# A scan, top-2 routing, an expert layer and its combination: three program blocks or one

## The chip, the cores and the metric

The kernel runs on one core of a Trainium2 chip. The metric is device time in microseconds (us) of one launch. The kernel before took 756.34 us, the median of three runs (754.75 to 756.58).

## The reference

The computation has five parts. The first two thirds of the time (a gated scan over 128 steps, relative-position attention with 16 heads, its output projection) are the same in both kernels. The changed part is the rest:

```python
# x: (32, 128, 128) after attention and residual; T = 128 steps, N = 32*128 = 4096 tokens, D = 128
xp = einsum('ntd,dh->nth', x, Wx) + b
h_t = tanh(xp_t + h_{t-1} @ Wh)                  # second scan, 128 steps, 32 sequences
p = softmax(h @ router_w.T)                      # 8 experts
w, idx = top_k(p, 2);  w = w / (w.sum() + 1e-9)
y_e = gelu(h @ W1_e.T + b1_e) @ W2_e.T + b2_e    # 128 -> 512 -> 128, exact gelu, expert e
out = x + sum over the two chosen e of w_e * y_e
```

Everything is float32.

## The kernel before, in words

A kernel is written as blocks. In a block each engine has its own instruction stream, and streams meet through semaphores. At the end of a block every engine executes a drain (listed on the line of the block, as L824) and then waits at a barrier for all others. The changed part is three blocks.

**Block 1 (L824 to L1047): second scan and routing.** The 128 steps are cut into 8 chunks of 16 steps, which are 512 tokens each. TensorE and ScalarE alternate on the scan: four matmul pairs by `wh2`, then a tanh (L918). While chunk m is scanned, chunk m-1 is routed: TensorE makes its logits and its transposed rows (L861), VectorE picks the two experts of each token, weighs them (L995 to L1002), counts positions per expert (L1008) and writes 8 columns of slot numbers, `slotu` (L1016). GpSimd then issues 8 scatters (L940), each of 128 rows of 129 floats (a token's state and the number of its output row) to its slot in the DRAM array `expert_inputs`. Each expert has its own region there. Per chunk:

```python
for k in range(2 * JT):
    pool.indirect_dma_start(xg_dram, ..., rows[o][:, k, :], None).then_inc(s_sc, 16)
pool.wait_ge(s_sc, (c + 1) * (16 * 2 * JT))
pool.sem_inc(s_scd, 1)
```

The wait (L942) and the increment (L943) let VectorE overwrite the row buffer. There are two buffers, `rows0` and `rows1`. After the eighth chunk VectorE makes the table of tiles `tab` (L1029 to L1047), and SP (the queue of the sync engine) writes 8 pieces of padding behind the experts' last rows (L847 to L852), one by one with a register load for each.

**Block 2 (L1082 to L1210): experts.** 72 tiles of 128 rows. A register load from `tab` gives the first row of a tile and its expert. SP loads the tile's rows into one of 8 buffers `xr` (L1090). TensorE transposes them (L1106), multiplies by the first weights (L1113) and by the second (L1130). ScalarE copies the expert's first weights (L1153) and does the gelu (L1144). VectorE copies the second weights (L1194) and adds the bias into `yr` (L1210). GpSimd scatters the 128 result rows to `expert_outputs` (L1173), at the row numbers that came with the tokens. The program has 8 tiles written out, a loop of 7 passes over 8 tiles, and 8 tiles written out again. The block ends when GpSimd has seen all scatters land (L1178 and L1179).

**Block 3 (L1221 to L1262): combination.** For each of 8 chunks SP loads both choices' results (two loads of 256 KB, L1231), VectorE adds them with their weights to the residual (8 operations, L1244), and ScalarE's queue writes 256 KB of output (L1260). A partition p holds the tokens j*128 + p of a chunk, so every row of these transfers is one token of 512 bytes.

The parts that the change touches, and what calls them:

Of the kernel before, what the change touches and what calls it, by code (L numbers as in the profile page):

```python
# [6 lines left out]
U32 = mybir.dt.uint32  # L7
I32 = mybir.dt.int32
ALU = mybir.AluOpType
# [3 lines left out]
P = 128  # L13
# [19 lines left out]
NS = 72  # L33
# [7 lines left out]
def build(nc, a):  # L41


    with ExitStack() as ctx:
# [760 lines left out]
        s_sc = sem("rows_scattered")  # L805
        s_scd = sem("chunk_scattered")
# [6 lines left out]
        VLINKS = 18  # L813

# [4 lines left out]
        def chunks(step):  # L819

            for m in range(NCH + 1):
                step(m, m < NCH, m >= 1)

        with nc.Block() as block:  # L824
            @block.sync
            def _(sp):
# [25 lines left out]
                sp.wait_ge(s_fill, 16 * E)  # L852

            @block.tensor
            def _(pe):
# [14 lines left out]
                def step(m, scan_on, route_on):  # L870
# [6 lines left out]
                    for j in range(TC):  # L877
# [9 lines left out]
                        if 2 <= j < 2 + JT:  # L887
                            k = j - 2
                            if k == 0:
                                pe.wait_ge(s_slot, c + 1)  # L890
                            tile = h2[o][:].rearrange("p t b -> p (t b)")[:, k * P:(k + 1) * P]
                            mm = column_products(2, k * E, (k + 1) * E, tile, rwT[:])
                            if k == JT - 1:
                                mm.then_inc(s_lg, 1)
                            mm = column_products(3, k * P, (k + 1) * P, tile, ident[:])
                            if k == JT - 1:
                                mm.then_inc(s_rt, 1)
                        if j == 12:
# [7 lines left out]
            @block.scalar  # L906
            def _(act):
                act.sem_inc(s_h2, 1)
                act.preload_act_table_set("exp_and_others")
                act.wait_ge(s_c2, 16)  # L910

                def step(m, scan_on, route_on):
                    r = m % 2
                    for j in range(TC):
                        if scan_on:
                            t = m * TC + j
                            act.wait_ge(s_r, t + 1)
                            act.activation(h2[r][:, j, :], ps[r][:, j * B:(j + 1) * B], ACT.Tanh,  # L918
                                           bias=cols[:, 5:6]).then_inc(s_h2, 1)
                        if route_on and j == 9:  # L920
                            act.wait_ge(s_ea, m)
                            act.activation(ex[:], lg[:], ACT.Exp).then_inc(s_eb, 1)

                chunks(step)

            @block.gpsimd
            def _(pool):
                pool.sem_inc(s_scd, 2)
                pool.wait_ge(s_rin, 144)
                pool.memset(ones[:], 1.0)  # L930
                pool.memset(pad[:, :, 0:D], 0.0)
                pool.tensor_copy(pad[:, :, D].bitcast(U32), padid[:]).then_inc(s_pad, 1)

                def step(m, scan_on, route_on):
                    if not route_on:
                        return
                    c, o = m - 1, 1 - m % 2
                    pool.wait_ge(s_slot, c + 2)
                    for k in range(2 * JT):
                        pool.indirect_dma_start(xg_dram, bass.IndirectOffsetOnAxis(slotu[o][:, k:k + 1], 0),  # L940
                                                rows[o][:, k, :], None).then_inc(s_sc, 16)
# [3 lines left out]
                chunks(step)  # L945

            @block.vector
            def _(dve):
                dve.sem_inc(s_slot, 1)
                dve.wait_ge(s_rin, 144)  # L950
                dve.wait_ge(s_pad, 1)
                dve.tensor_copy(offs[:, 0, :], ebase[:]).then_inc(s_init, 1)
                dve.wait_ge(s_init, 1)

                def step(m, scan_on, route_on):
                    if not route_on:
                        return
                    c, o = m - 1, 1 - m % 2
                    k = [0]

                    def link(op):
                        k[0] += 1
                        op.then_inc(s_v, 1)
                        dve.wait_ge(s_v, c * VLINKS + k[0])

                    def over_e(v):
                        return v.unsqueeze(len(v.shape)).broadcast_to([*v.shape, E])

                    dve.wait_ge(s_lg, c + 1)
                    link(dve.tensor_copy(lgc[:], ps[2][:, 0:JT * E].rearrange("p (j e) -> p j e", e=E)))  # L970
                    dve.tensor_reduce(small[:, 0, :], lgc[:], AX.X, ALU.max)
                    for j in range(JT):
                        op = dve.max(top[:, j, :], lgc[:, j, :])
                    link(op)

                    dve.tensor_tensor(lg[:], lgc[:], over_e(small[:, 0, :]), ALU.subtract).then_inc(s_ea, 1)
                    for j in range(JT):
                        op = dve.max_index(topi[:, j, :], top[:, j, :], lgc[:, j, :])
                    link(op)
                    link(dve.tensor_copy(topf[:], topi[:]))  # L980
                    for x in range(2):
                        op = dve.tensor_tensor(sel[:, x], iota[:].unsqueeze(1).broadcast_to([P, JT, E]),
                                               topf[:, :, x:x + 1].broadcast_to([P, JT, E]), ALU.is_equal)
                    link(op)
                    dve.tensor_tensor(both[:], sel[:, 0], sel[:, 1], ALU.add).then_inc(s_sel, 1)

                    dve.wait_ge(s_rt, c + 1)
                    dve.wait_ge(s_scd, c + 1)
                    for x in range(2):
                        dve.tensor_copy(rows[o][:, x * JT:(x + 1) * JT, 0:D], ps[3][:].rearrange("p (j d) -> p j d", d=D))  # L990
                    link(dve.tensor_copy(rows[o][:, :, D].bitcast(U32), destf[:]))
                    link(dve.tensor_scalar(destf[:], destf[:], float(BANK), None, ALU.add))

# [322 lines left out]
```

## Time and profile before

| | us |
|---|---|
| median of three runs | 756.34 |
| the profiled execution, its own time | 756.94 |
| its span, first to last instruction | 755.1 |
| TensorE busy in the span | 577.0 |
| VectorE, ScalarE, GpSimd busy | 428.5, 402.4, 394.1 |
| block 1: span from | 443.1 |
| block 2: span from | 574.6 |
| block 3: span from | 727.5 |

Times in the trace are microseconds from the start of the span. Busy times are sums over instructions and do not say what waits for what. An instruction with a letter q behind its engine (POOLq, SPq) is a sequencer's: a drain, a semaphore or the issue of a transfer. The end of a scatter on GpSimd (POOL) is the end of its issue; its landing comes later and is listed apart. A row of a source line gives the instruction, how often it ran, its shortest, median and longest duration in ns, and the start of the first and the last.

### The profile page before, as it was taken

The numbers are of one execution on the slowest core, as the hardware profiler recorded it, in microseconds if no ns is written. First come the engines' busy times: TensorE is split into PE (matmuls) and PEld (weight loads), VectorE is DVE, ScalarE is ACT, GpSimd is POOL, SyncE is SP. The second block draws the span as 40 slices with busy tenths as digits, with TensorE's granted clock in tenths as the row PEclk, the third lists the DMA queues.
The fourth block names the chain that finished last, engine by engine and source line by source line (L and its number), as shares of the span: only waits on it lengthen the run. The fifth ranks groups of instructions, "written<-read, shape, count | busy, mean of one in ns | idle before, by whom it ended". The sixth has DMA issues, their size and how long they took to land. (4 is left out here: it accounts for less than half of the span.)

```text
span 755.1 us, 26992 instructions
## 1 busy us (share of the span) xinstructions
PE 577.0 (76%) x10048; PEld 442.5 (59%) x10048; DVE 428.5 (57%) x1998; ACT 402.4 (53%) x1129; POOL 394.1 (52%) x436
## 2 busy tenths in 40 slices
PE   3888888888679989999999666776403999999900
PEld 1655565565556666667767433333203999999900
DVE  1666666666357678777785423645631555555517
ACT  4666666666205555555556243444203999999800
POOL 3454454455148688888886101656660555555510
PEclk9999999999979999999999785756555999999955
DMA  6365565565756666676653027111121222222238
GB/s 238 131 232 200 205 230 191 189 231 189 251 145 193 183 186 195 178 195 193 197 170 115 1 69 229 48 42 45 44 74 36 68 70 68 70 70 70 57 106 235
DMA packets 124140, 106.41 MB, mean 141 GB/s; under 512 B 9216, under 2 KB 100864, under 8 KB 123776
## 3 DMA queue, kind: packets, MB, share of 16 engines
q1 hardware_dynamic: 115456, 93.88, 40.0%
q0 software_dynamic: 4352, 8.95, 3.6%
q10 hardware_dynamic: 4224, 2.10, 0.9%
q8 instruction: 73, 1.20, 0.7%
q14 instruction: 35, 0.29, 0.2%
HBM read 57.15 MB, written 45.65 MB: 136 GB/s over the span
## 5 line engine op out<-in xcount | busy, mean ns | idle before, releaser
L473 POOL TENSOR_TENSOR sc<-sc,mx 128x1024 f32<-128x1024 f32 x64 | 121.3, 1897 | 55.6 <-DVE mx L613 55.6
L383 POOL TENSOR_SCALAR QD<-q_all,mask 128x128 f32<-128x128 f32 x128 | 89.5, 712 | 98.3 <-DVE pre L348 95.0
L613 DVE CUSTOM_DVE_ANT_0 sc<-banks,s2t 128x128 f32<-128x128 f32 x512 | 113.0, 286 | 47.1 <-PE banks L523 46.8
L1173 POOL DMA_INDIRECT expert_outputs<-yr,xr x72 | 72.1, 1001 | 80.0 <-DVE yr L1210 75.2
L662 ACT ACTIVATE PT<-banks 128x512 f32<-128x512 f32 x128 | 69.7, 595 | 76.6 <-PE banks L538 76.3
L940 POOL DMA_INDIRECT expert_inputs<-rows,slotu x64 | 61.9, 967 | 52.5 <-DMA expert_inputs<-rows,slotu 19.6
L339 DVE COPY s2stage<-banks 128x512 f32<-128x512 f32 (+1 forms) x90 | 76.6, 852 | 16.5 <-PE banks L248 16.5
L1144 ACT ACTIVATE hid<-banks,w1b 128x128 f32<-128x128 f32 x288 | 82.3, 369 | 4.2 <-PE banks L1113 4.2
L248 PE MATMUL banks<-RK,QD 32*128 32x128 f32 x1024 | 78.5, 454 | 4.0 <-DVE s2stage L339 0.9
L1113 PE MATMUL banks<-xt,w1b 128*128 128x128 f32 x576 | 77.8, 279 | 0.0
L1130 PE MATMUL banks<-w2b,hid 128*128 128x128 f32 x576 | 76.4, 276 | 0.3 <-ACT hid L1144 0.3
L538 PEld LDWEIGHTS banks<-ident,sc 128*128 128x128 f32 x512 | 55.5, 142 | 29.5 <-issue 19.7
L1113 PEld LDWEIGHTS banks<-xt,w1b 128*128 128x128 f32 x576 | 71.7, 196 | 0.0
L538 PE MATMUL banks<-ident,sc 128*128 128x128 f32 x512 | 70.7, 281 | 0.5 <-issue 0.5
L1130 PEld LDWEIGHTS banks<-w2b,hid 128*128 128x128 f32 x576 | 70.4, 193 | 0.5 <-ACT hid L1144 0.5
L348 DVE TENSOR_TENSOR_SCAN pre<-xz,gl 128x64 f32<-128x64 f32 x128 | 37.5, 293 | 53.8 <-ACT gl L300 50.6
L215 PEld LDWEIGHTS banks<-hs,wh 128*32 128x32 f32 x1016 | 25.6, 140 | 71.0 <-ACT hs L303 71.0
L248 PEld LDWEIGHTS banks<-RK,QD 32*128 32x128 f32 x1024 | 61.1, 318 | 9.8 <-issue 6.6
L918 ACT ACTIVATE h<-banks,cols 128x32 f32<-128x32 f32 x128 | 36.8, 288 | 56.1 <-PE banks L861 56.1
L215 PE MATMUL banks<-hs,wh 128*32 128x32 f32 x1016 | 42.6, 251 | 28.7 <-ACT hs L303 25.4
L861 PE MATMUL banks<-h,wh 128*32 128x32 f32 x1024 | 40.0, 236 | 30.5 <-ACT h L918 30.4
L1194 DVE TENSOR_SCALAR w2b<-w2all 128x640 f32 x72 | 38.6, 536 | 42.7 <-issue 42.1
(121 smaller groups left out, 1001.5 us busy)
## 6 DMA issues: line engine op xcount, KB each, us to landing
s_scratch<-s2stage SPq DMA_DIRECT2D x32, 1024.0 KB, 4.9
s2t<-s_scratch SPq DMA_DIRECT2D x64, 512.0 KB, 4.6
xr<-expert_inputs SPq DMA_DIRECT2D x72, 64.5 KB, 1.8
xz<-in_xz SPq DMA_DIRECT2D x8, 512.0 KB, 5.9
yb<-expert_outputs SPq DMA_DIRECT2D x16, 256.0 KB, 4.8
KB<-k_all SPq DMA_DIRECT2D x32, 64.0 KB, 3.4
q_all<-in_xT SPq DMA_DIRECT2D x1, 2048.0 KB, 9.0
w1a<-in_w1T SPq DMA_DIRECT2D x1, 2048.0 KB, 8.8
```

What stands on the lines that cost most here:

```text
L215: mm = pe.matmul(ps[bank][at, lo:hi], w[:, at], moving, start=first, stop=last, tile_position=(0, 32 * c), skip_group_check=True)
L248: mm = pe.matmul(ps[4 + j][:, tl * T:(tl + 1) * T], QD[G % 3][32 * j:32 * j + 32, tl].rearrange("p h b -> p (h b)"), relk_window(j, t), st ...
L339: dve.tensor_copy(stage[G % SETS][:, lo:hi].rearrange("p g q k -> p (g q k)"), banks[:, (4 + lo) * BANK:(4 + hi) * BANK]).then_inc(s_s2c, 1)
L383: op = pool.tensor_scalar(QD[G % 3][:, :, h, :], q_all[:, :, quad(G)].rearrange("p b t -> p t b"), mask[:, h:h + 1], None, ALU.mult)
L473: pool.tensor_tensor(sc[U % RING][:], sc[U % RING][:], mx[U % RING][:].unsqueeze(2).broadcast_to([P, HH, T]), ALU.subtract)\
L538: mm = pe.transpose(blocked[:, j // 2, j % 2], sc[U % RING][:, 4 * x + j, :], ident[:])
L613: op = dve.tensor_tensor_reduce(out=sc[r][:, h, :], in0=ps[2 * (U % 2) + h // 4][:, h % 4 * T:(h % 4 + 1) * T], in1=s2t[r][:, h, :], scale ...
L662: act.activation(pairs[:, 2 * (2 * u + x):2 * (2 * u + x) + 2], ps[4 + x][:].rearrange("p (a r) -> p a r", a=2), ACT.Exp, scale=DH ** -0.5 ...
L1113: mm = pe.matmul(ps[2 + k % 2][:, f * P:(f + 1) * P], w1b[k % 2][:, f * P:(f + 1) * P], xt[k % 2][:], start=True, stop=True)
L1130: mm = pe.matmul(ps[4 + k % 2][:, 0:D], hid[k % 2][:, f, :], w2b[k % 2][:, f * D:(f + 1) * D], start=(f == 0), stop=(f == FC - 1))
L1144: op = act.activation(hid[k % 2][:, f, :], ps[2 + k % 2][:, f * P:(f + 1) * P], ACT.Gelu, bias=w1b[k % 2][:, FF + f:FF + f + 1])
L1173: pool.indirect_dma_start(yg_dram, bass.IndirectOffsetOnAxis(xr[k][:, D:].bitcast(U32), 0), yr[k][:], None).then_inc(s_ys[k], 16)
```

## The change

- The three blocks become one. Where a block ended, engines now wait for semaphores: SP waits for all padding, all scatters and the table before it loads the first tile, and for all result scatters before it loads the first results.
- GpSimd no longer waits for a chunk's scatters. `rows_scattered` becomes two semaphores, one for each row buffer, and VectorE waits for the scatters of the chunk before the last one when it reuses the buffer.
- For the last chunk the order changes: TensorE makes the four logits ahead of the four transposed rows; ScalarE copies the rows; VectorE computes the slots, then the table, and only then the weights of the two choices.
- ScalarE's queue issues four of the eight paddings. Its gelu table is loaded behind the scan.
- 71 tiles in place of 72. The last seven are written out behind the loop.
- A partition now holds tokens 4p to 4p+3 of a chunk at the end: `destf` numbers the output rows so, each partition's row of a combination transfer is 2 KB in one piece, and the host puts the token order right by a transpose.

```diff
-NS = 72
+NS = 71
-        s_sc = sem("rows_scattered")
-        s_scd = sem("chunk_scattered")
+        s_sc = [sem(f"rows_scattered{i}") for i in range(2)]
...
             @block.sync
             def _(sp):
...
                 sp.wait_ge(s_end, 1)
                 sp.sem_inc(s_spass2, 1)
-                for e in range(E):
-                    end = sp.value_load(ends[0:1, e:e + 1], min_val=0, max_val=E * CAP - P)
-                    sp.dma_start(xg_dram[bass.ds(end, P), :], pad[:, e, :]).then_inc(s_fill, 16)
+                for e in range(0, E, 2):
+                    fill(sp, e)
                 sp.wait_ge(s_fill, 16 * E)
+                for o in range(2):
+                    sp.wait_ge(s_sc[o], NCH // 2 * 16 * 2 * JT)
+                sp.wait_ge(s_tab, TLINKS)
...
+                for k in range(RX - 1):
+                    load(NS // RX, k, True)
+
+                for k in range(RX):
+                    sp.wait_ge(s_ys[k], 16 * (NS // RX + (k < NS % RX)))
+                yin = yg_dram[0:2 * N, :].rearrange("(x c p j) d -> c x p j d", x=2, j=JT, p=P)
...
             @block.tensor
...
+                            if scan_on:
+                                logits(j - 2)
+                                rows_of(j - 2)
+                            elif j == 2:
+                                for k in range(JT):
+                                    logits(k)
+                                for k in range(JT):
+                                    rows_of(k)
...
             @block.scalar
...
+                        if route_on and not scan_on and j == 8:
+                            act.wait_ge(s_last, 1)
+                            act.wait_ge(s_rt, m)
+                            for x in range(2):
+                                op = act.activation(rows[1 - r][:, x * JT:(x + 1) * JT, 0:D],
+                                                    ps[3][:].rearrange("p (j d) -> p j d", d=D), ACT.Copy)
+                            op.then_inc(s_rows, 1)
...
+                act.preload_act_table_set("gelu_and_others")
+                act.wait_ge(s_end, 1)
+                act.sem_inc(s_apass2, 1)
+                for e in range(1, E, 2):
+                    fill(act, e)
+                act.wait_ge(s_tab, TLINKS)
+                act.wait_ge(s_win, 16 * (3 + E))
...
             @block.gpsimd
...
                     pool.wait_ge(s_slot, c + 2)
+                    if not scan_on:
+                        pool.wait_ge(s_rows, 1)
                     for k in range(2 * JT):
                         pool.indirect_dma_start(xg_dram, bass.IndirectOffsetOnAxis(slotu[o][:, k:k + 1], 0),
-                                                rows[o][:, k, :], None).then_inc(s_sc, 16)
-                    pool.wait_ge(s_sc, (c + 1) * (16 * 2 * JT))
-                    pool.sem_inc(s_scd, 1)
+                                                rows[o][:, k, :], None).then_inc(s_sc[o], 16)
...
-                for k in range(RX):
-                    pool.wait_ge(s_ys[k], 16 * (NS // RX))
...
             @block.vector
...
+                    def last_rows():
+                        dve.wait_ge(s_sc[o], c // 2 * 16 * 2 * JT)
+                        dve.tensor_copy(rows[o][:, :, D].bitcast(U32), destf[:]).then_inc(s_last, 1)
...
+                    if scan_on:
+                        state_rows()
+                        weights()
+                        slots()
+                    else:
+                        slots()
+                        dve.wait_ge(s_slot, c + 2)
+                        table()
+                        weights()
+                        return
...
-        "dest": (np.arange(2)[None, :, None] * N + np.arange(JT)[None, None, :] * P
-                 + np.arange(P)[:, None, None]).reshape(P, 2 * JT).astype(np.float32),
+        "dest": (np.arange(2)[None, :, None] * N + np.arange(JT)[None, None, :]
+                 + np.arange(P)[:, None, None] * JT).reshape(P, 2 * JT).astype(np.float32),
```

How the instructions stand, at three places. First GpSimd from the sixth chunk's scatters to the first result scatter, before (a line is a source line, the operation, what it writes and reads, and the semaphores that it waits for):

```order
L940 DMA expert_inputs<-rows1,slotu1 34816x129 [waits rows_scattered,rows_and_slots_ready]
L940 DMA expert_inputs<-rows1,slotu1 34816x129 x7
L940 DMA expert_inputs<-rows0,slotu0 34816x129 [waits rows_scattered,rows_and_slots_ready]
L940 DMA expert_inputs<-rows0,slotu0 34816x129 x7
L940 DMA expert_inputs<-rows1,slotu1 34816x129 [waits rows_scattered,rows_and_slots_ready]
L940 DMA expert_inputs<-rows1,slotu1 34816x129 x7
L824 UNCONDITIONAL_BRANCH [waits rows_scattered]
L1168 UNCONDITIONAL_BRANCH [waits barrier_Pool_Activation_PE_DVE_SP_gather]
L1173 DMA expert_outputs<-yr0,xr0 10240x128 [waits tile_outputs_ready]
```

and in the changed kernel:

```order
L1121 DMA expert_inputs<-rows1,slotu1 34688x129 [waits rows_and_slots_ready]
L1121 DMA expert_inputs<-rows1,slotu1 34688x129 x7
L1121 DMA expert_inputs<-rows0,slotu0 34688x129 [waits rows_and_slots_ready]
L1121 DMA expert_inputs<-rows0,slotu0 34688x129 x7
L1121 DMA expert_inputs<-rows1,slotu1 34688x129 [waits last_state_rows_copied,rows_and_slots_ready]
L1121 DMA expert_inputs<-rows1,slotu1 34688x129 x7
L1129 DMA expert_outputs<-yr0,xr0 10112x128 [waits tile_outputs_ready]
```

The wait for `rows_scattered` at each chunk and the branch with the barrier are gone; the last chunk waits for ScalarE's copy of the rows.

Second, SP from the last tile load to the first load of results, before:

```order
L1090 DMA xr7<-expert_inputs 128x129
L1094 REGISTER_ALU
L1094 COMPARE_AND_BRANCH
L1082 UNCONDITIONAL_BRANCH
L1222 UNCONDITIONAL_BRANCH [waits barrier_Pool_Activation_PE_DVE_SP_release]
L1225 UNCONDITIONAL_BRANCH
L1225 ISA
L1231 ISA [waits second_choice_added]
L1231 DMA yb0<-expert_outputs 128x4x128
```

and in the changed kernel:

```order
L906 DMA xr6<-expert_inputs 128x129
L919 UNCONDITIONAL_BRANCH [waits tile_outputs_scattered4,tile_outputs_scattered5,tile_outputs_scattered3,tile_outputs_scattered6,tile_outputs_scattered2,tile_outputs_scattered7,tile_outputs_scattered1,tile_outputs_scattered0]
L919 ISA
L925 ISA [waits second_choice_added]
L925 DMA yb0<-expert_outputs 128x512
```

The barrier's release is replaced by waits for the scatters themselves, and a load's rows are 512 floats in one piece.

Third, VectorE behind the last chunk's choices, before:

```order
L985 TENSOR_TENSOR both<-sel 128x32 [waits routing_chain]
L990 COPY rows1<-banks 128x4x128 [waits chunk_scattered,state_rows_ready]
L990 COPY rows1<-banks 128x4x128
L991 CAST rows1<-destf 128x8
L992 TENSOR_SCALAR destf<-destf 128x8 [waits routing_chain]
L995 TENSOR_REDUCE small<-ex 128x4 [waits router_exp_ready,routing_chain]
L996 TENSOR_TENSOR exs<-sel,ex 128x64
L997 TENSOR_REDUCE er<-exs 128x8 [waits routing_chain]
L998 TENSOR_TENSOR small<-er 128x4 [waits routing_chain]
```

and in the changed kernel:

```order
L1242 TENSOR_TENSOR both<-sel 128x32 [waits routing_chain]
L1215 TENSOR_TENSOR offs<-offs,banks 128x8 [waits positions_ready]
L1215 TENSOR_TENSOR offs<-offs,banks 128x8 [waits routing_chain] x3
L1216 TENSOR_TENSOR pos<-banks,offs 128x32 [waits routing_chain]
L1218 COPY offs<-offs 128x8 [waits routing_chain]
L1219 TENSOR_TENSOR exs<-sel,pos 128x64
L1220 TENSOR_REDUCE slotf<-exs 128x8 [waits routing_chain]
L1222 CAST slotu1<-slotf 128x8 [waits slot_numbers_ready]
L1152 CAST ends<-offs 128x8 [waits rows_and_slots_ready]
```

The copies of the rows have left VectorE, and the weights (L995 to L1002 before) stand behind the table.

## Rows read from the trace of the kernel before

**Rows 1.** Windows: stretch; busy PE, PEld, DVE, ACT, POOL; clock; DMA share, GB/s

```profile
569.00:575.00 6.00, 0.00 (x0) 0.00 (x0) 0.00 (x0) 0.23 (x1) 0.00 (x0) 0.50 0.00 0
583.00:718.00 135.00, 134.42 (x1203) 134.03 (x1202) 72.31 (x211) 124.27 (x353) 70.76 (x71) 1.00 0.25 67
718.00:728.00 10.00, 0.00 (x0) 0.00 (x0) 0.09 (x1) 0.00 (x0) 1.31 (x2) 0.57 0.05 14
```

**Rows 2.** Lines L943, L824; timeline (start, length, instruction): the first block's end

```profile
L943 POOLq EVENT_SEMAPHORE  x8: 17/17/17, 481.1 to 569.1; - x8
...
L824 POOLq DRAIN  x1: 5280/5280/5280, 569.2 to 569.2; - x1
L824 SPq EVENT_SEMAPHORE  x1: 17/17/17, 574.6 to 574.6; - x1
...
575.41 8.09 SPq L1090 DMA_DIRECT2D xr<-expert_inputs  x8
```

**Rows 3.** Line L1082: the second block's end

```profile
L1082 POOLq DRAIN  x1: 5943/5943/5943, 721.4 to 721.4; - x1
L1082 SPq EVENT_SEMAPHORE  x1: 17/17/17, 727.5 to 727.5; - x1
```

**Rows 4.** Timeline, GpSimd's scatters; in brackets the idle time ahead

```profile
469.21 1.18 POOL L940 DMA_INDIRECT expert_inputs<-rows,slotu  x1 [15.85 <-DVE slotu L1016]
...
541.67 0.96 POOL L940 DMA_INDIRECT expert_inputs<-rows,slotu  x1 [0.30 <-issue]
544.76 0.95 POOL L940 DMA_INDIRECT expert_inputs<-rows,slotu  x1 [2.13 <-DMA expert_inputs<-rows,slotu]
...
551.07 1.36 POOL L940 DMA_INDIRECT expert_inputs<-rows,slotu  x1 [0.31 <-issue]
...
566.78 0.96 POOL L940 DMA_INDIRECT expert_inputs<-rows,slotu  x1 [0.30 <-issue]
```

**Rows 5.** Timeline around the last two chunks: VectorE and SP

```profile
537.94 0.17 DVE L1016 CAST slotu<-slotf 128x8 uint32<-128x8 f32 x1
...
540.95 0.19 DVE L970 COPY lgc<-banks 128x32 f32<-128x32 f32 x1 [2.84 <-PE banks L861]
...
548.84 0.17 DVE L1016 CAST slotu<-slotf 128x8 uint32<-128x8 f32 x1
...
550.39 8.41 SPq L851 DMA_DIRECT2D expert_inputs<-pad  x8
...
554.30 0.23 DVE L1047 CAST tab<-tabf 128x144 int32<-128x144 f32 x1
```

**Rows 6.** Line L940 of the source, all 64 scatters: idle time, times

```profile
  DMA expert_inputs<-rows,slotu: 19.6, 7
...
DMA to landing us min/median/max: 2.3/2.3/3.7
```

**Rows 7.** Windows of 1 us behind the first tile (clock: third number from the end)

```profile
581.00:582.00 1.00, 1.00 (x7) 1.00 (x7) 0.46 (x2) 0.88 (x5) 0.00 (x0) 0.50 0.23 54
...
583.00:584.00 1.00, 1.00 (x11) 1.00 (x11) 0.30 (x2) 0.88 (x5) 0.00 (x0) 1.00 0.29 66
```

**Rows 8.** Timeline, the results of two tiles, one after the other

```profile
636.78 0.29 DVE L1210 TENSOR_TENSOR yr<-banks,w2b 128x128 f32<-128x128 f32 x1 [0.27 <-PE banks L1130]
...
638.68 0.29 DVE L1210 TENSOR_TENSOR yr<-banks,w2b 128x128 f32<-128x128 f32 x1 [0.27 <-PE banks L1130]
```

**Rows 9.** Timeline of the combination

```profile
727.95 15.74 SPq L1231 DMA_DIRECT2D yb<-expert_outputs  x16
732.03 1.14 DVE L1244 SCALAR_TENSOR_TENSOR x1r<-yb,wts,x1r 128x128 f32 x4 [13.94 <-DMA yb<-expert_outputs]
...
735.42 1.14 DVE L1244 SCALAR_TENSOR_TENSOR x1r<-yb,wts,x1r 128x128 f32 x4 [0.96 <-DMA yb<-expert_outputs]
```

**Rows 10.** Windows: the combination's loads, and the weights' loads in block 1

```profile
727.90:744.00 16.10, 0.00 (x0) 0.00 (x0) 10.21 (x37) 0.00 (x0) 0.00 (x0) 0.50 0.93 262
...
450.00:460.00 10.00, 6.37 (x152) 3.26 (x152) 0.17 (x1) 3.96 (x14) 2.11 (x3) 0.50 1.04 357
```

More of the change, by code:

```diff
@@ L813, in build @@
         VLINKS = 18
+        TLINKS = 10
         def before(r, j):
@@ L904, in _ @@
                 chunks(step)
[L906 to L940, printed above, removed]
-                                                rows[o][:, k, :], None).then_inc(s_sc, 16)
-                    pool.wait_ge(s_sc, (c + 1) * (16 * 2 * JT))
-                    pool.sem_inc(s_scd, 1)
-                chunks(step)
@@ L1082, in build @@
-        with nc.Block() as block:
-            @block.sync
-            def _(sp):
-                def load(i, k, reused):
-                    first = sp.value_load(tab[0:1, 1, bass.ds(i * RX + k, 1)], min_val=0, max_val=E * CAP + (NULL - 1) * P)
-                    if reused:
-                        sp.wait_ge(s_ys[k], i * 16)
-                        sp.sem_inc(s_lpass, 1)
-                    sp.dma_start(xr[k][:], xg_dram[bass.ds(first, P), :]).then_inc(s_xr[k], 16)
-                for k in range(RX):
-                    load(0, k, False)
-                with sp.Fori(1, NS // RX) as i:
-                    for k in range(RX):
-                        load(i, k, True)
-            @block.tensor
-            def _(pe):
@@ L1166, in _, with step @@
                 over_tiles(act, step)
+                with act.Fori(0, NCH // 2) as i:
+                    for r in range(2):
+                        c = i * 2 + r
+                        act.wait_ge(s_o1, c + 1 + RY)
+                        act.sem_inc(s_apass, 1)
+                        act.dma_start(a["out"].rearrange("(c p j) d -> c p j d", j=JT, p=P)[bass.ds(c, 1)]
+                                      .rearrange("c p j d -> (c p) j d"), x1r[:, bass.ds(c * JT, JT), :])\
+                           .then_inc(s_out[r], 16)
+                for r in range(2):
+                    act.wait_ge(s_out[r], 16 * (NCH // 2))
             @block.gpsimd
             def _(pool):
+                pool.wait_ge(s_rin, 144)
+                pool.memset(ones[:], 1.0)
+                pool.memset(pad[:, :, 0:D], 0.0)
+                pool.tensor_copy(pad[:, :, D].bitcast(U32), padid[:]).then_inc(s_pad, 1)
+                def step(m, scan_on, route_on):
+                    if not route_on:
+                        return
+                    c, o = m - 1, 1 - m % 2
+                    pool.wait_ge(s_slot, c + 2)
+                    if not scan_on:
+                        pool.wait_ge(s_rows, 1)
+                    for k in range(2 * JT):
+                        pool.indirect_dma_start(xg_dram, bass.IndirectOffsetOnAxis(slotu[o][:, k:k + 1], 0),
+                                                rows[o][:, k, :], None).then_inc(s_sc[o], 16)
+                chunks(step)
                 def step(i, k, s, has_next, has_second):
@@ L1182, in _ @@
+                chunks(step)
+                dve.wait_ge(s_win, 16 * (3 + E))
                 dve.sem_inc(s_xt, 2)
```

333 lines of the change are left out of this document (177 added, 156 removed).

## The prediction

> **What bounds the kernel now.** I read the windows first. Between 583 and 718 TensorE is busy 134.42 of 135 us at the full granted clock of 1.00: the expert tiles are bound by TensorE, and only fewer tiles or a start at another time can move that stretch. Ahead of it and behind it lie stretches in which nothing is busy: 569 to 575, and 718 to 728 but for 1.3 us of GpSimd [rows 1]. They are the place to look. Then I asked the timeline and the source lines what stands in them. At 569.1 the last of eight semaphore increments behind the scatters passes (L943): all rows have landed. GpSimd's sequencer then shows a drain that lasts 5.28 us, SP passes the barrier at 574.6, and the first tile load is issued at 575.41 [rows 2]. The second hole has the same form: a drain on GpSimd from 721.4 for 5.94 us, release at 727.5 [rows 3].
>
> What is ahead of 569.1 is GpSimd's stream of scatters, at 469.21 to 566.78 [rows 4]. It is the last thing that block 1 finishes: VectorE's table is ready at 554.53 and SP's paddings are issued by 558.8 [rows 5]. In this stream one scatter starts 1.26 us after the other (544.76 to 551.07 is five of them), and seven times GpSimd waits 2.1 us or more for a landing, 19.6 us in all [rows 4, 6]. So the critical path of this third of the program is: scan, slots, scatters, landing, drain, tiles on TensorE, last scatter's landing, drain, combination.
>
> **The change part by part.**
>
> *No wait per chunk.* The 19.6 us don't all come back, since the slots of a chunk are known only when the scan has got there. The last chunk but one has its slots at 537.94 + 0.17 = 538.11 [rows 5]; GpSimd comes to them 0.3 us later, the step between instructions when nothing is waited for [rows 4], at 538.4. By then it has no backlog: the first scatter of all starts at 469.21 and this one six chunks and 69.2 us later, 11.5 us each, and a chunk of scatters without a wait takes 8 x 1.262 = 10.1. So it starts the last chunk at 548.5 and its last scatter at 548.5 + 7 x 1.262 = 557.3, where the kernel before has 566.78. **Gain 9.5.** Bounds: 9.0, if VectorE's table operations stretch a scatter more than they did (one took 1.36 in place of 0.96, while the table was made [rows 4]); 9.5 above, as the scan isn't touched.
>
> What could be late next is the last chunk's slot numbers. Before, they took from 540.95 to 549.01, which would be 0.5 later than 548.5 [rows 5]. The new order takes the copies of the rows and the weights out of that chain, so they are early. The order of the last chunk is worth 0.5 at most; I take 0 beyond the 9.5 (which assumes it). ScalarE's two copies have from about 541 to 548.5. The table took 5.5 us behind the slots [rows 5] and, even at the old place (554.5), would be early for a landing near 559.6. The paddings took 8.41 us on one queue, behind 549.01 by 1.4 [rows 5]: at the old place and on one queue they would land around 561, about 1 us late; on two queues and a few us earlier they are hidden with over 4 us to spare. VectorE's new wait for the chunk before last costs nothing: those scatters are issued by about 526.6 + 10.1 = 536.7, landed 2.3 later [rows 6], 539, and VectorE idles until 540.95 [rows 5].
>
> [...]
>
> *Block 1's end.* Landed at 569.1, barrier 574.6, first load 575.41 [rows 2]. Of the 6.3 us, 0.8 (register load and issue) stay; the drain is no longer between. SP waits for the same semaphore increments that GpSimd saw. Landing: 557.3 + 2.3 = 559.6; first load at 560.4 or 560.5. **Gain 5.5**, bounds 5.0 to 5.5. The gelu table (ScalarE) and the first weights, which stood behind the barrier too, are ready in the wait. The rest of the start stays: TensorE comes cold and runs at half clock until about 583 (0.50 at 581, 1.00 at 583 [rows 7]). Its idle time ahead is some 14 us shorter, and I give that no gain: bounds 1 us either way.
>
> *71 tiles.* One tile is 638.68 - 636.78 = 1.90 [rows 8]. **Gain 1.9**, as the stretch is full [rows 1].
>
> *Block 2's end.* GpSimd's eight waits are passed just ahead of its drain at 721.4; SP's release is 727.5 [rows 3]. SP now waits itself. Its instructions from release to the first load (0.45 us, 727.5 to 727.95 [rows 3, 9]) stay. 727.5 - 721.3 = 6.2. **Gain 6.2**, bounds 5.5 to 6.5. GpSimd still has a drain at the very end. Both drains have the same length per scatter: 5.28/64 and 5.94/72 are 82.5 ns each [rows 2, 3]. If that is a debt which grows with each scatter, the single one now covers 64 + 71 = 135 and takes 11.1 us. It begins behind the issue of the last scatter, about 703, and is over at 714, while the combination runs until about 731: hidden by 17 us. If the combination were under 11 us, it would show.
>
> *2 KB rows.* The loads ran at 262 GB/s at a DMA share of 0.93, which is 282 per full share; the weights' loads, in rows of 2 KB, at 357 and 1.04, which is 343 [rows 10]. The first pair of loads lands 4.1 us after its issue (727.95 to 732.03), and VectorE then waits once more, 0.96 (735.42) [rows 9]. After that VectorE is never kept waiting, so speed there gives nothing. Of the 4.1, 524 KB are 1.9 us at 282 and 1.5 at 343: 0.3 or 0.4. With the 0.96 and nothing for the last output: **gain 1.3**, bounds 0 (loads no faster; other traffic is the limit) and 2.3 (1 us more at the last output).
> The Trainium skill speaks against it: DMA: Bandwidth & Descriptors, "Why small descriptors are slow (HBM only)", puts a fixed cost of about 3 cycles on each packet and finds joining them worthwhile only up to 256 B. By its count, an estimate, 2 KB is 67 cycles where four of 512 B are 76, 12% less; the term would be about 1.1.
>
> **Sum.** 9.5 + 5.5 + 1.9 + 6.2 + 1.3 = 24.4. The profiled execution took 756.94 (span 755.1), so 732.5; that execution is 0.6 above the median of the three runs, so the median after could as well be 732.0. I say 732.5. The bounds of the terms add to 20.4 (with 1 us lost at the start of the tiles) and 26.7 (with 1 us won there): 730 to 736.5.
>
> **The rivals.**
> 1. *GpSimd pays its debt inside.* The drain may be work that must be done some time, at the latest when some store is full. The trace shows 72 scatters in a row without a drain, none shows 135. If 5.3 us of it came due among the scatters of block 1, they would be on the path: 737.8. Among the tiles it would be hidden: GpSimd is busy 70.8 of 135 us [rows 1]. Against it: no scatter between two drains is longer than 1.36 us before.
> 2. *The scatters queue up.* Without the waits, the rate may be set by something else (transfers in flight), so that the mean pace stays at one chunk in 12.7 us and the stream ends as before. Then the 9.5 is lost: 742.0. For it: landings of up to 3.7 us [rows 6]. Against: within a chunk the pace is 1.26 from first to last, with two or three in flight.
> 3. *Slower: TensorE stays at the low clock.* TensorE now comes to the tiles after a shorter idle time and in another phase. The clock rose within 6 us of the first tile before, and stayed [rows 1, 7]. At 0.50 a tile costs about 1.9 us more (its 1.9 us are all TensorE time). The gain of 24.4 is used up by 13 such tiles beyond those before; with 71 of them the kernel would take about 865. Nothing in this trace shows the clock fall while TensorE is fully busy.
> 4. *The change isn't what it says:* the landing that SP waits for is seen later than GpSimd saw it, so that a hole of 5 us stays at each end: 743.
>
> **How the numbers follow.** The forecast 0.84 (730 to 736.5), rival 1 0.05, rival 2 0.04, rival 4 0.03, rival 3 and anything else that is as bad 0.04. The range of 8 in 10, 729.5 to 738, holds the forecast's and rival 1. All cases but the last are faster by more than 0.3% (2.3 us, about what a measurement here can tell from no change): faster 0.95, same 0.01, slower 0.04.
>
> **What would show it.** Scatters 1.26 us apart with only short gaps of about 1.4 between chunks, none between the last two; the last starting near 557.3. First tile load near 560.5. Tiles 1.90 us apart, clock 1.00 from about 569. First result load near 704.9, 0.5 behind the last landing. One drain on GpSimd, near 11 us, over long before the end. VectorE's combination without the 0.96 wait. The prediction is wrong if the sixteen last scatters don't stand in one row, if a hole over 2 us is left at either old block end, or if the tiles' pitch has changed.

## The result

The changed kernel takes 731.22 us (median of 4 runs, 730.53 to 735.28), the kernel before 755.92 beside it (median of 4). The ratio is 0.9687, 95% interval 0.9654 to 0.9720: 24.7 us less, where 732.5 and a gain of 24.4 had been forecast. The profiled execution, from which the rows below come, is the slowest of the four (735.28, span 733.3). It differs from the profile before also ahead of the changed part: the slots of the last chunk but one are ready at 540.50, not 538.11, 2.39 us that have to do with no step of the change. So the terms are read as differences between marks.

The windows, in the columns of [rows 1], from the first tile to the last and of the second old block end:

```profile
560.00:568.00 8.00, 2.21 (x9) 1.92 (x10) 0.68 (x3) 0.00 (x0) 0.95 (x1) 0.50 0.18 48
568.00:702.00 134.00, 134.00 (x1190) 134.00 (x1189) 71.54 (x209) 123.92 (x351) 68.06 (x69) 0.99 0.24 67
705.00:708.00 3.00, 0.00 (x0) 0.00 (x0) 0.00 (x0) 0.00 (x0) 0.96 (x1) 0.95 0.13 44
```

The long stretch is as full as before and at the full clock. The empty stretches at its ends are shorter. The timeline of VectorE, SP and GpSimd over the last two chunks, which answers to [rows 4, 5]:

```profile
540.33 0.17 DVE L1222 CAST slotu<-slotf 128x8 uint32<-128x8 f32 x1
540.77 0.96 POOL L1121 DMA_INDIRECT expert_inputs<-rows,slotu  x1 [1.79 <-DVE slotu L1222]
...
546.45 0.32 DVE L1222 CAST slotu<-slotf 128x8 uint32<-128x8 f32 x1
548.14 4.13 SPq L867 DMA_DIRECT2D expert_inputs<-pad  x4
549.61 1.39 POOL L1121 DMA_INDIRECT expert_inputs<-rows,slotu  x1 [0.31 <-issue]
551.30 0.96 POOL L1121 DMA_INDIRECT expert_inputs<-rows,slotu  x1 [0.30 <-issue]
552.00 0.29 DVE L1170 CAST tab<-tabf 128x142 int32<-128x142 f32 x1
560.15 0.95 POOL L1121 DMA_INDIRECT expert_inputs<-rows,slotu  x1 [0.30 <-issue]
563.32 2.60 SPq L906 DMA_DIRECT2D xr<-expert_inputs  x3
565.19 0.47 PE L999 MATMUL banks<-ident,xr 128*128 128x128 f32 x1 [20.46 <-DMA xr<-expert_inputs]
```

Sixteen scatters stand in one row from 540.77. The last chunk's slots come at 546.77, 4.5 us before GpSimd starts its first scatter (551.30); the table and the paddings are early too. What GpSimd waits for over all 64 scatters, to be read beside [rows 6] (idle time in us, times):

```profile
  DVE slotu L1222: 27.5, 7
...
DMA to landing us min/median/max: 2.3/2.4/4.4
```

The 19.6 us for landings are gone, and GpSimd waits for slot numbers instead: 16.85 us ahead of the first chunk (15.85 before), and 1.3 to 2.3 ahead of each of the six that follow. It has no backlog until the scan is over. Then the end of the tiles, and the one drain that is left (line of the block; count, duration in ns, start):

```profile
705.04 0.96 POOL L1129 DMA_INDIRECT expert_outputs<-yr,xr  x1 [0.54 <-issue]
707.81 14.38 SPq L925 DMA_DIRECT2D yb<-expert_outputs  x16
711.36 1.14 DVE L1301 SCALAR_TENSOR_TENSOR x1r<-yb,wts,x1r 128x128 f32 x4 [7.13 <-DMA yb<-expert_outputs]
...
713.99 1.14 DVE L1301 SCALAR_TENSOR_TENSOR x1r<-yb,wts,x1r 128x128 f32 x4 [0.20 <-DMA yb<-expert_outputs]
```

```profile
L869 POOLq DRAIN  x1: 7700/7700/7700, 704.8 to 704.8; - x1
```

Before, the first result load stood 9.05 us behind the start of the last scatter (718.90 to 727.95). Now it is 2.77. The drain is issued to the sequencer before the last scatter has run, and is over at 712.5, 21 us before the end.

| from, to | before | after | second profile (e5) | forecast gain | gain, after / e5 |
|---|---|---|---|---|---|
| slots of chunk 6, last scatter's start | 28.67 | 19.65 | 19.63 | 9.5 | 9.02 / 9.04 |
| last scatter, first tile load | 8.63 | 3.17 | 3.14 | 5.5 | 5.46 / 5.49 |
| first tile load, last result scatter | 143.49 | 141.72 | 141.87 | 1.9 | 1.77 / 1.62 |
| last result scatter, first result load | 9.05 | 2.77 | 2.76 | 6.2 | 6.28 / 6.29 |
| first result load, end of span | 27.15 | 25.49 | 26.05 | 1.3 | 1.66 / 1.10 |
| sum | | | | 24.4 | 24.19 / 23.54 |

The interval of the ratio allows 21.2 to 26.2 us, the terms add to 24.19 and 23.54, and the part ahead of the change moved by 2.39 us between two executions. So 24.7 so close to 24.4 is in part luck; the terms one by one are the better test.

### The profile page after: what moved, and what is told of

The parts are those of the page before. It is cut to its first block and busy times, and to the rows that moved or that the text cites. A ratio compares the mean times of both kernels' runs of the same rounds, so it can differ in the third digit from the quotient of the medians.

```text
span 733.3 us, 26881 instructions
## 1 busy us (share of the span) xinstructions
PE 577.5 (79%) x10031; PEld 442.6 (60%) x10031; DVE 425.1 (58%) x1992; ACT 401.4 (55%) x1126; POOL 392.5 (54%) x435
## 5 line engine op out<-in xcount | busy, mean ns | idle before, releaser
L538 PEld LDWEIGHTS banks<-ident,sc 128*128 128x128 f32 x512 | 56.2, 143 | 28.6 <-issue 18.9
L215 PEld LDWEIGHTS banks<-hs,wh 128*32 128x32 f32 x1016 | 25.5, 140 | 71.1 <-ACT hs L303 71.1
```

Of the source, the lines that this page charges most:

```text
L538: mm = pe.transpose(blocked[:, j // 2, j % 2], sc[U % RING][:, 4 * x + j, :], ident[:])
```

## The experiments

They ran in three groups on three chips: A (e1 to e4), B (e5 to e8), C (e9 to e12). Ratios are to the kernel before on the same chip: 809.26 us on A, 754.94 on B, 804.91 on C. So chips differ by 50 to 54 us for the same program, and nearly all of that lies between the first scatter and the last (see the end).

### e1 and e9: only the wait per chunk taken out of the kernel before

```diff
-                    pool.wait_ge(s_sc, (c + 1) * (16 * 2 * JT))
-                    pool.sem_inc(s_scd, 1)
...
-                    dve.wait_ge(s_scd, c + 1)
+                    if c >= 2:
+                        dve.wait_ge(s_sc[o], c // 2 * 16 * 2 * JT)
```

(`s_sc` becomes two semaphores, and GpSimd waits for both at the end of the block.)

> The three blocks of the kernel before are kept; only GpSimd's wait per chunk is taken out (two semaphores, one per row buffer; GpSimd waits for all scatters once, at the end of block 1). My theory (the scatters run at 1.26 us each from the slots of the last chunk but one): last scatter 9.0 to 9.5 us earlier, but VectorE's table and SP's eight paddings now follow: paddings issued by about 558 and landed about 560, against a landing of the scatters near 560, so the whole gain is 8.5 to 9.5 us and the drain of some 5 us stays. Rival (the scatters queue up, their pace is set by transfers in flight): gain 0 to 2.

> The kernel before with GpSimd's wait per chunk taken out and nothing else, as in the first group, now perhaps on a chip on which TensorE doesn't stall in the scan. If the chunks' slots come every 11.5 us: last scatter 9.0 to 9.5 us earlier, time 8 to 9.5 shorter (the single queue of eight paddings may end last). If they come every 19.8 us, as in the first group: no gain, since the wait of 12.7 us per chunk was hidden. Rival of the first: pace of the scatters set by transfers in flight, gain 0 to 2 where the slots come every 11.5 us.

Measured: 810.69 on A, ratio 1.0004 (0.9981 to 1.0027), and 804.49 on C, ratio 0.9996 (0.9976 to 1.0016). No gain, twice. The first scatters of chunks 1, 2 and 7 in e1's timeline:

```profile
490.23 0.96 POOL L938 DMA_INDIRECT expert_inputs<-rows,slotu  x1 [9.74 <-DVE slotu L1015]
509.91 0.96 POOL L938 DMA_INDIRECT expert_inputs<-rows,slotu  x1 [9.87 <-DVE slotu L1015]
...
608.31 0.96 POOL L938 DMA_INDIRECT expert_inputs<-rows,slotu  x1 [8.96 <-DVE slotu L1015]
```

On these chips a chunk's slots come every 19.8 us, not every 11.5. A chunk of scatters with its wait takes 12.7, so GpSimd has no backlog even with the wait, and a wait that is taken out moves only idle time from one releaser to another. The rival (scatters queue up) would give the same times, but not these rows: GpSimd waits 9 to 10 us for slots. Where the slots are held up is seen in e3's timeline of TensorE (same chip), in the first steps of a chunk in which logits and rows are made beside the scan:

```profile
547.00 0.28 PE L935 MATMUL banks<-rwT,h 128*32 128x8 f32 x8
547.11 1.53 PE L935 MATMUL banks<-ident,h 128*32 128x128 f32 x8
553.41 0.34 PE L935 MATMUL banks<-h,wh 128*32 128x32 f32 x8 [4.78 <-issue]
...
554.48 1.15 PE L935 MATMUL banks<-ident,h 128*32 128x128 f32 x5 [0.22 <-issue]
```

and at the same place of a chunk on chip B (e5):

```profile
493.05 0.33 PE L935 MATMUL banks<-h,wh 128*32 128x32 f32 x8
493.17 0.28 PE L935 MATMUL banks<-rwT,h 128*32 128x8 f32 x8
493.28 0.63 PE L935 MATMUL banks<-ident,h 128*32 128x128 f32 x8
493.79 0.34 PE L935 MATMUL banks<-h,wh 128*32 128x32 f32 x8
```

TensorE stands still for 4.78 us and the trace names no releaser. Two steps of the scan, 546.88 to 556.40, take 9.52 us here and 1.48 on B: 8 us more, about what the slots are late by in each chunk (19.8 less 11.5). It comes in every chunk on A and C and in none on B, 3 to 6 us behind the first scatter of a chunk, where the logits and rows are made. In some chunks the trace books the stall to ScalarE's tanh. That TensorE's instructions come late is a guess; none of the runs shows the cause.

What follows: the term of 9.5 could not be had alone on these chips, since its premise, slots at 11.5 us a chunk, doesn't hold there. For chips like B it rests on traces of the whole change: from chunk 6's slots to the last scatter they have 19.65 (the result's profile) and 19.4 to 19.7 us (e5 to e8), where the kernel before has 28.67. No run on B takes out the wait alone.

### e2: the changed kernel with the wait per chunk put back

```diff
+                    pool.wait_ge(s_sc[o], (c // 2 + 1) * 16 * 2 * JT)
```

> The changed kernel with one part undone: GpSimd waits again for each chunk's scatters. My theory: last scatter 9 us later than in the changed kernel, time +9, near 740.5. Rival (the gain at the block's end comes from starting later work, not from the scatters): +0 to 3.

Measured on A: 794.47, ratio 0.9833 (0.9801 to 0.9865). The first scatter of the last chunk starts at 601.66, 0.77 us behind its slots (600.72 + 0.17); without the wait, in e3, 0.28 behind them. So it costs 0.5 at this place, and 0.5 to 0.8 in each chunk between the first and the last. But the next slots then come later too: from the first chunk's slots to the seventh's e2 takes 121.8 us, and the six traces on A and C without the wait and with the old place of the logits (e1, e3, e4, e9, e10, e11) take 118.0 to 119.1. From chunk 6's slots to the last scatter e2 takes 0.9 more than e3. Against e3 that makes 4.0 by the traces (3.1 and 0.9). By the times it is 4.1: the medians are 3.2 apart, and e3's short rows cost it 0.9 besides (see below). The scatter of the times is of the same order. In e1 and e9 the same wait was worth nothing, with intervals that leave 2 us. Why the slots follow the scatters in e2 isn't shown. So +9 did not come, for want of a backlog, and what came lies just above the rival's 3.

e2 is 14.8 us faster than the kernel before without the removal that the prediction priced highest, and e3, which has it, 18.0; where the gain comes from, e4 and e10 tell.

### e3: 512-byte rows again, e4: the last chunk in the old order, e10: both

```diff
-                yin = yg_dram[0:2 * N, :].rearrange("(x c p j) d -> c x p j d", x=2, j=JT, p=P)
+                yin = yg_dram[0:2 * N, :].rearrange("(x c j p) d -> c x p j d", x=2, j=JT, p=P)
```

(e3; `destf` and the output go back with it.)

```diff
-                    if scan_on:
-                        state_rows()
-                        weights()
-                        slots()
-                        assert k[0] == VLINKS, k
-                    else:
-                        slots()
-                        dve.wait_ge(s_slot, c + 2)
-                        table()
-                        weights()
-                        return
+                    state_rows()
+                    weights()
+                    slots()
+                    assert k[0] == VLINKS, k
```

(e4; TensorE's and ScalarE's parts of the order go back with it.)

> The changed kernel with rows of 512 bytes at the end as before (loads, output and row numbers). My theory: the combination is 1.5 to 1.7 us longer (first pair of loads 0.5, the second wait 0.8, last output 0.2). Rival (the packet rule, 12% of the transfer time): 0.2 to 0.4 longer.

> The changed kernel with the last chunk in the old order (logits and rows by turns, VectorE copies the rows, weights ahead of the slots, table behind). My theory: the last chunk's slots come 4 to 5 us later, which uses up the 4.1 us that they were early for GpSimd, so the time is 0 to 1 us longer. Rival (the last chunk's slots are on the path): 4 to 5 us longer.

> The changed kernel with two parts undone, which lie in different stretches of the trace: the last chunk in the old order, and rows of 512 bytes at the end. Where TensorE doesn't stall: the last chunk's slots come 4 to 5 us later, its scatters 0 to 1 us later; the combination is 1.5 to 1.7 us longer; together +1.5 to 2.7. Where it stalls: the order alone 4 to 5 us. Rival (the packet rule): the combination only 0.2 to 0.4 longer.

Measured: e3 791.26, ratio 0.9781 (0.9758 to 0.9804); e4 794.65, 0.9832 (0.9811 to 0.9853), both on A; e10 791.85 on C, 0.9837 (0.9803 to 0.9870).

Rows: from the first result load to the end e3 takes 26.43 us, e10 26.35; e4 and e2, which have the 2 KB rows, 25.5 each. The rows are worth 0.9, between the 1.5 to 1.7 expected and the rival's 0.2 to 0.4. The single traces scatter: with long rows e8 has 25.3 and e5 26.05, with short ones e9 26.6 and e1 26.7. In e3 the first addition starts 3.99 behind the first load, in the profiles with long rows 3.45 to 3.60. The rest of what after's profile gained over [rows 9] is scatter between executions, as e5's 26.05 shows.

Order: the slots of the last two chunks in e3's timeline and in e4's.

```profile
583.69 0.17 DVE L1222 CAST slotu<-slotf 128x8 uint32<-128x8 f32 x1
597.60 0.17 DVE L1222 CAST slotu<-slotf 128x8 uint32<-128x8 f32 x1
```

```profile
588.14 0.17 DVE L1212 CAST slotu<-slotf 128x8 uint32<-128x8 f32 x1
606.89 0.17 DVE L1212 CAST slotu<-slotf 128x8 uint32<-128x8 f32 x1
```

13.91 us between them in the new order, 18.75 in the old. GpSimd waits for the last chunk's slots here, so all 4.8 are on the path, as e4's rival had it; the medians have 3.4 between e4 and e3, which with the 0.9 of the rows is 4.3. On chip B the slots are over 4 us early, so by the trace the order is worth at most the 0.5 of the forecast; no run there undoes it. The same edit is worth next to nothing on one chip and 4.8 us on another.

e10 leaves of the change the missing wait, the two block ends and the tile. It is 13.1 us faster than the kernel before; the forecast's terms without the wait, which e9 shows to be worth nothing on this chip, are 5.5 + 6.2 + 1.9 = 13.6. The interval allows 10.5 to 15.9.

### e5: the changed kernel once more

No edit, run beside e6 to e8.

> The changed kernel once more, on the chip of this group of runs, so that the others have it beside them. If TensorE's scan has no stalls here: 24 us faster than before (ratio 0.968), the last 16 scatters in one row. If TensorE stalls in the scan as in the group before (8 us in each chunk, ends of stalls put down to issue): about 18 us faster (ratio 0.978), since the scatters' waits were then hidden by the scan.

Measured: 731.22, ratio 0.9684 (0.9665 to 0.9704), 23.7 us less: the first of the two cases. Its marks are in the table above.

### e6: the drain at the very end, e7: the combination in a block of its own

```diff
+                pool.wait_ge(s_o1, NCH + RY)
```

(e6: GpSimd, behind its last result scatter, waits for VectorE's last addition. e7 moves SP's, ScalarE's and VectorE's parts of the combination into a second block, ahead of which GpSimd waits for all result scatters.)

> The changed kernel with one more wait: GpSimd waits for the last addition of the combination ahead of the end of the block, so that its drain can only begin 25 us behind its last scatter. Theory A (the drain does work that is owed for the scatters, whenever it is called): a drain of 5 to 11 us behind the last addition, the kernel 3 to 9 us longer. Theory B (something runs for 6 to 7 us behind the last scatter by itself, and the drain only waits for its end): a drain of under 0.1 us and no change of time.

> The changed kernel with the combination in a block of its own again; GpSimd waits for its scatters there. My theory: a drain of 5.3 us or more on GpSimd between the last landing and the first load, +6.2 us. By the debt of 82.5 ns per scatter (135 scatters) the drain would be 11.1 us and the time +11.5. Rival (the gap was the block's change itself, not the drain): the gap is there, but the drain ends well before it.

Measured: e6 735.30, ratio 0.9736 (0.9712 to 0.9760); e7 739.30, 0.9788 (0.9766 to 0.9810). The drains, e6's and e7's:

```profile
L869 POOLq DRAIN  x1: 6508/6508/6508, 730.7 to 730.7; - x1
```

```profile
L869 POOLq DRAIN  x1: 6517/6517/6517, 705.4 to 705.4; - x1
```

e6 asks for the drain at 730.7, where e5 does at 701.1, and it still takes 6.51 us. GpSimd idles in between, so the work isn't done by itself; it is done when the drain asks for it. At the end of the program nothing hides it: 4.1 us more. That is theory A. In e7 the drain stands between the landing and the barrier, as in [rows 3]:

```profile
702.83 0.96 POOL L1106 DMA_INDIRECT expert_outputs<-yr,xr  x1 [0.54 <-issue]
712.53 3.20 SPq L1282 DMA_DIRECT2D yb<-expert_outputs  x6
```

9.70 us from scatter to load, where e5 has 2.76: 6.9 more by the trace, 8.1 by the times (1.6 us of the two profiles' difference stand ahead of chunk 6's slots, which e7 doesn't touch). That is the block end's price, undone by itself, and the drain fills it, so the rival is out. But the drain behind 64 + 71 scatters takes 6.51, not the 11.1 of 135 x 82.5 ns.

### e8 and e12: slots ahead of the weights in every chunk

```diff
-                        if j == 2:
+                        if j == 0:
...
-                        if j == 12:
+                        if j == 9:
...
-                        weights()
                         slots()
+                        weights()
```

(e8: logits and rows are made two steps of the scan earlier, the counts at step 9. e12 has the counts at step 8, the last chunk as in the changed kernel.)

> The changed kernel with earlier slot numbers in chunks 1 to 7: logits and rows two scan steps earlier, position counts at step 9 in place of 12, VectorE computes slots ahead of the weights, the exponential at step 7. My theory (the last 16 scatters start with the last but one chunk's slots and set the start of the tiles): slots 2.9 us earlier, time 2.9 us shorter than the changed kernel, as the last chunk's slots were 4.1 us early. Rival (the last chunk's slots take over): 0 to 1.5 us shorter.

> The kernel with earlier slot numbers again, with the position counts at scan step 8 in place of 9 (in the run before VectorE waited 0.8 us for them). From the start of the block to the first tile load: 0.7 us shorter than there and 2.0 us shorter than in the changed kernel. Rival (the last chunk's slots take over from the backlog of scatters): no change against the run with step 9.

Measured: e8 730.57 on B, ratio 0.9684 (0.9660 to 0.9708), the same as e5. e12 783.63 on C, 0.9735 (0.9702 to 0.9767).

From the block's first load to the first tile load e8 takes 116.52 us and e5 117.78: 1.3 less. VectorE now waits for the counts in e8:

```profile
533.52 0.75 DVE L1215 TENSOR_TENSOR offs<-offs,banks 128x8 f32<-128x8 f32 x4 [0.81 <-PE banks L935]
```

The gain is too small for the times to show. It lies in the rival's range, but not for its reason: the last chunk's slots are ready at 543.33, still 2.3 us ahead of their first scatter (545.65). The slots themselves came only 1.1 us earlier, counted from the block's first load, where 2.9 were expected. On C earlier slots are worth more, as GpSimd waits for them in every chunk: over the same stretch e12 takes 168.3 us (440.33 to 608.58), e10 176.1, of which difference the last chunk's order is some 4.8. e12 has the lowest ratio of any whole kernel on A and C, but the changed kernel itself was not timed on those chips; e3, with 0.9 to come for its rows, is the nearest, and e12 is not shown to beat it. Its expectation compares with e8 and the changed kernel on the same chip, which no run has, and stays open.

### e11: 39 tiles in place of 71

```diff
-            with eng.Fori(1, NS // RX) as i:
+            with eng.Fori(1, NX // RX) as i:
```

(`NX = 39` sets the number of tiles on every engine. Thirty-two tiles aren't computed, and the combination reads another array.)

> The changed kernel with 39 of the 71 tiles, and the combination reads another array of the same size: 32 tiles and with them part of the result are left out. Tiles: 32 x 1.896 = 60.7 us shorter than the changed kernel. The drain of GpSimd, counted from the end of the last scatter, after 64 + 39 = 103 scatters: 8.5 us if each scatter adds 82.5 ns without end; 6.5 us if the debt has a ceiling (it was 5.28 after 64, 5.94 after 72, 6.51 after 135); 3.9 us if it is taken off in the middle and starts anew (135 less 56 is 79, which 82.5 ns turn into 6.51).

Measured on C: 723.33. From the first tile load to the last result scatter it takes 81.6 us, where e10 and e12 on the same chip take 144.6 and 144.5: 63 us for 32 tiles, not 60.7. The question was what a drain costs behind 64 + 39 = 103 scatters. Line of the block, and the last scatter:

```profile
L870 POOLq DRAIN  x1: 9663/9663/9663, 695.8 to 695.8; - x1
```

```profile
695.99 0.96 POOL L1130 DMA_INDIRECT expert_outputs<-yr,xr  x1 [0.54 <-issue]
```

The drain ends at 705.4, which is 8.5 us behind the end of the last scatter (696.95). 103 x 82.5 ns are 8.50. So 64, 72 and 103 scatters lie on one line (e1 and e9, with 5.29 and 5.93, lie on it too), and there is no ceiling at 6.5. With 135, what is left at the end are 6.51 us (e6), the price of 79, on B and on A and C alike.

One place in the traces answers to this. GpSimd's scatters of the 49th, 50th and 51st tile in the changed kernel, which are the 113th to 115th of all, and those of the 49th and 50th tile in the kernel before:

```profile
664.20 1.13 POOL L1129 DMA_INDIRECT expert_outputs<-yr,xr  x1 [1.30 <-DVE yr L1289]
667.16 1.09 POOL L1129 DMA_INDIRECT expert_outputs<-yr,xr  x1 [1.83 <-DVE yr L1289]
668.56 0.96 POOL L1129 DMA_INDIRECT expert_outputs<-yr,xr  x1 [0.30 <-issue]
```

```profile
676.16 1.13 POOL L1173 DMA_INDIRECT expert_outputs<-yr,xr  x1 [1.30 <-DVE yr L1210]
677.70 0.96 POOL L1173 DMA_INDIRECT expert_outputs<-yr,xr  x1 [0.41 <-issue]
```

A scatter starts 0.81 us behind the end of its rows' addition on VectorE. The 114th starts 2.23 us behind it, and GpSimd has caught up three tiles later, while VectorE keeps its pitch of 1.9. All ten profiles with 135 scatters have this at the same scatter, whatever the chip and the time that has passed; the kernel before, e1 and e9 (a drain behind 64) and e11 (103 in all) have it nowhere. So something is done between the 113th and the 114th. In this profile it takes at most the 1.83 us that GpSimd idles, not the 4.6 of 56 scatters, so it isn't shown that this is the whole of what the drain lacks.

## Why the prediction was right

**No wait per chunk.** Right but for its size: 9.02 for 9.5, at the lower bound of 9.0. The missing half is the step "starts the last chunk at 548.5": GpSimd is 0.3 us behind the slots at 540.77 as forecast, but its eighth scatter takes 1.39 us in place of 0.96 while the table is made, and the last starts 19.38 behind the first (15 x 1.262 are 18.9). In the second profile it is one of the sixteen too, 1.38 us. No run on B takes out the wait alone, so the 9.0 is read from traces. That the wait's 19.6 us don't come back whole was the point of this step, and A and C show it in full: with slots every 19.8 us nothing comes back in e1 and e9.

**The slots, the table and the paddings are early.** Right in the profiles without the stall: the slots 4.5 us ahead of their first scatter, the table over and the last padding issued by 552.3, 10 us ahead of the last scatter's landing. On the slow-scanning chips the slots of the last chunk are what is late, and there the order carries 4.8.

**Block 1's end** 5.46 for 5.5, **71 tiles** 1.77 for 1.9, **block 2's end** 6.28 for 6.2. e7 undoes the last by itself (6.9 by the trace), and e10 times the three together, 13.1 for 13.6. TensorE starts at half clock as before; the granted clock is 1.00 again from about 571, 6 us behind the first tile's matmul at 565.2, and before it rose at 583, 5.5 behind 577.3. With the 2.4 us by which this execution runs late, that is the 569 of the forecast, and the bounds of 1 us for the start were not needed.

**2 KB rows.** 1.3 was right in size, and its parts only roughly: 1.66 and 1.10 in the two profiles, 0.9 undone on A and C. The first pair lands 0.5 sooner (3.55 us for 4.08), and the second wait goes from 0.96 to 0.20, or to 0.71 in e5. By the Trainium skill, DMA: Bandwidth & Descriptors, "Why small descriptors are slow (HBM only)", the prediction made it about 1.1, an estimate (12% of 1.9 us and the 0.96 are rather 1.2), and the runs don't part that from 1.3.

**The drain.** The one figure that fell, and it was hidden, so the time doesn't show it: 11.1 us forecast, 7.70 seen, of which 6.5 lie behind the last scatter. That a debt of 82.5 ns grows with each scatter is borne out to 103 of them; "covers 64 + 71 = 135" is what failed. The price of 56 scatters is missing from the drain. Rival 1 (GpSimd pays inside) is thus half right: the one irregular place, ahead of the 114th scatter, lies among the tiles, where 1.4 us of delay are hidden, and not among block 1's scatters. That the pause is the payment, and what starts it, is not shown.

**The other rivals.** Scatters don't queue up: sixteen in a row keep 1.26 to 1.27 us but for the one of 1.39, though a landing now takes up to 4.4. TensorE's clock is 0.99 over 568 to 702. The forecast called itself wrong if a hole over 2 us were left at an old block end. From the end of the last scatter's issue to the first load it is 2.2 us at the first (561.10 to 563.32) and 1.8 at the second (706.00 to 707.81). The sign was drawn too tight: the forecast's own 558.3 to 560.5 is 2.2 as well. What is left is the landing, with no drain in it, and not the 5 us of rival 4.

## What to carry to other kernels

A wait taken out pays only for the stretch in which its engine has a backlog: count from the last input that it can't have earlier, not by the sum of the waits. A block's end behind indirect scatters costs their landing and then GpSimd's drain, 82.5 ns for each scatter up to the 103 seen here, with every other engine held; put the next stage into the same block behind the semaphores that it needs, and let the drain fall where nobody waits. Take a second chip before you call a part of a change worthless, since on another one the bound can lie elsewhere, here at most 0.5 by the trace against 4.8 us for the same order.

## What was not expected of the hardware

- The same program takes 755 us on some chips and 805 to 809 on others. Nearly all of it lies in the second scan and the routing of its last chunk: in e9 the stream of scatters goes from 468.22 to 614.40, 146.2 us, where [rows 4] have 97.6. TensorE is idle there for up to 5.7 us at a time (e3) with no releaser in the trace.
- GpSimd's drain isn't a wait for transfers in flight: asked for when all results have long been read (e6), it still takes 6.51 us. Behind 64, 72, 103 and 135 scatters it takes 5.28, 5.94, 8.5 and 6.51, counted from the end of the last scatter where it was asked for earlier.
- Ahead of the 114th scatter since the last drain GpSimd pauses: it starts 2.23 us behind its input in place of 0.81, in every profile that has so many.
